# Second attention's preparation moved between the last expert tiles, its bias as one product, and the last layer's norms behind a later split

## What is computed

```
x = x + L0_xattn(layernorm(x), ctx)   # one nearest context row is taken per token
x = x + L0_ffn(layernorm(x))          # 8 experts, top 2 per token, gelu
x = x + L1_xattn(layernorm(x), ctx)   # the "second attention", below
x = x + L1_ffn(layernorm(x))          # the "last layer": experts choose tokens

# L1_xattn, 16 heads of 64
xn = layernorm(x) * gamma + beta
q  = xn @ w_q;  k, v = split(ctx @ w_kv)
o  = softmax(q * 64**-0.5 @ k.T) @ v
return (o @ w_out + b_out) * tanh(gate)
```

## Time and profile before

| | us |
|---|---|
| median of 3 runs (lowest, highest) | 1761.12 (1756.11, 1764.85) |
| profiled execution, its own time | 1759.72 |
| its span in the trace | 1757.8 |
| PE busy (share of the span) | 1659.3 (94%) |
| DVE busy | 1311.6 (75%) |
| ACT busy | 1131.0 (64%) |
| POOL busy | 792.0 (45%) |

### The profile page before, as it was taken

One profiled execution on the slowest core, in us unless ns is written; L12 is line 12 of the kernel. 1 busy time (PEld: TensorE's weight loads), 2 busy tenths in 40 slices (PEclk: granted clock), 3 DMA queues, 4 the chain that ended last, 5 costly groups with the idle time before them and its releaser, 6 DMA issues.

```text
span 1757.8 us, 40697 instructions
## 1 busy us (share of the span) xinstructions
PE 1659.3 (94%) x15617; PEld 1414.3 (80%) x15621; DVE 1311.6 (75%) x2861; ACT 1131.0 (64%) x2880; POOL 792.0 (45%) x1125
## 2 busy tenths in 40 slices
PE   7999999999999999999999879999999999997768
PEld 4677776678788999999999768888888888886656
DVE  5899998461816889888898467878887888767557
ACT  1477776424347778778787467778777877764330
POOL 3245432120012333333331477888788878755300
PEclk9899999899999999999999989999999999999899
DMA  7857565146876677767776722232223222211378
GB/s 207 230 122 152 123 133 147 49 162 231 309 258 223 239 257 247 249 244 246 252 247 236 243 73 64 71 97 71 67 72 95 73 67 68 79 62 49 101 235 291
DMA packets 138770, 283.08 MB, mean 161 GB/s; under 512 B 13808, under 2 KB 89968, under 8 KB 125904
## 3 DMA queue, kind: packets, MB, share of 16 engines
q1 hardware_dynamic: 118176, 168.89, 32.1%
q0 software_dynamic: 20400, 111.59, 18.7%
HBM read 199.03 MB, written 81.13 MB: 159 GB/s over the span
## 4 chain that ended last, share of the span: by engine, by line
PE 70%; DVE 7%; POOL 6%; DMA 5%; issue 5%; ACT 5%; SPq 0%; POOLq 0%; DVEq 0%; ACTq 0%
PE ps L1344 12%; PE ps L1358 11%; PE ps L407 5%; PE ps L2201 5%; PE ps L243 4%; PE ps L2186 3%; PE ps L2224 3%; ACT P L220 3%; PE ps L411 3%; PE ps L500 3%; PE ps L476 3%; POOL P L233 2%; PE ps L488 2%; PE ps L2237 2%; PE ps L576 2%
## 5 line engine op out<-in xcount | busy, mean ns | idle before, releaser
L220 ACT ACTIVATE P<-ps,NM 128x256 f32<-128x256 f32 x512 | 238.0, 495 | 116.4 <-DVE NM L209 116.4
L233 POOL TENSOR_TENSOR P<-P,RS 128x1024 f32<-128x1024 f32 x128 | 244.7, 1918 | 56.4 <-DVE RS L227 55.8
L1344 PE MATMUL ps<-XRP,W1P 128*128 128x256 f32 (+1 forms) x1872 | 226.2, 281 | 3.3 <-DVE W1P L1428 3.3
L1344 PEld LDWEIGHTS ps<-XRP,W1P 128*128 128x128 f32 x1872 | 219.8, 190 | 4.1 <-DVE W1P L1428 3.6
L1358 PE MATMUL ps<-W2P,HP 128*128 128x256 f32 x1704 | 204.2, 278 | 0.0
L1358 PEld LDWEIGHTS ps<-W2P,HP 128*128 128x128 f32 x1704 | 200.3, 188 | 0.0
L642 DVE TENSOR_REDUCE NM<-ps 128x2 f32<-128x512 f32 x256 | 164.4, 684 | 31.0 <-PE ps L476 30.2
L741 ACT ACTIVATE PT<-ps 128x512 f32<-128x512 f32 x256 | 139.2, 597 | 63.8 <-PE ps L488 61.5
L209 DVE TENSOR_REDUCE NM<-ps 128x2 f32<-128x512 f32 x256 | 164.0, 682 | 3.9 <-PE ps L2186 3.1
L1277 POOL DMA_INDIRECT WE<-in_we,WIX x39 | 44.3, 1136 | 265.3 <-DVE W1P L1428 192.2
L243 PE MATMUL ps<-CST,P 128*128 128x128 f32 x1024 | 139.3, 279 | 17.8 <-ACT PT L250 16.7
(11 more groups left out here) (287 smaller groups left out, 3685.6 us busy)
## 6 DMA issues: line engine op xcount, KB each, us to landing
KS<-k_scratch SPq DMA_DIRECT2D x64, 256.0 KB, 3.0
V<-v_scratch SPq DMA_DIRECT2D x16, 1024.0 KB, 6.9
k_scratch<-KVM SPq DMA_DIRECT2D x52, 256.0 KB, 3.2
QS<-q_scratch SPq DMA_DIRECT2D x96, 128.0 KB, 4.5
v_scratch<-KVM SPq DMA_DIRECT2D x40, 256.0 KB, 2.8
ctx_scratch<-CHL SPq DMA_DIRECT2D x32, 256.0 KB, 2.8
CHR<-ctx_scratch SPq DMA_DIRECT2D x16, 512.0 KB, 4.8
ys_scratch<-YS SPq DMA_DIRECT2D x32, 256.0 KB, 7.9
```

Source lines behind the costliest of these rows:

```text
L220: i = e.activation(self.P[u % 4][:, c, :], PS[SB1[n % 4]][:, y * 256:y * 256 + 256], ACT.Exp, bias=self.NM[:, u % 4, c:c + 1], accum_out=s ...
L233: e.tensor_tensor(p, p, self.RS[:, u % 4, :].unsqueeze(2).to_broadcast([128, 4, 256]), ALU.mult).then_inc(self.s_pn, 1)
L1344: m = e.matmul(PS[p][:, hh * 256:hh * 256 + n], W1P[i % 2][wi][:, cc * 1024 + hc * 128:cc * 1024 + hc * 128 + 128], XRP[i % 2][xi][:, cc * ...
```

## The change

- SP issues the loads of gamma and beta (GB), bias (BO), gate (TG) and W1O's source (WT1) in the expert stage, behind the store of expert tile 37 (the next to last), ahead of the last context loads. Before, the first three followed the last ys store and WT1 the last value store. WT1 gets another place in memory.
- ScalarE makes tanh(gate), W1O's high parts and the first two keys' high parts between value tiles 113 to 121. VectorE makes W1O's low parts before the first queries' low part.
- Queries 0 go ahead of tile 127. Queries 1 get a bank of their own and need not wait for the low part of queries 0; their high part is made behind the first slot's exponentials.
- Statistics of batch 1 and two of its adds come earlier. Its norms move from slot 0 to slot 1, its two transposes and scales from slots 0 and 1 to slots 1 and 2; adds and gathers of batches 2 and 3 move accordingly.
- The bias is one product: ROW2 has ones in rows 0 and 32, and the bias's high part lies in row 0 of BOS, the low part in row 32. It is made in slot 1.
- Norm b of the last layer, from b = 5 on, waits for one batch's split more.

```diff
@@ sp_ffn, behind the store of tile NTF - 2
                 w.wait_ge(s_ym, NTF - 1)
+                e.dma_start(GB[:, :, :], A["gb"]).then_inc(d_w0_w1, 16)
+                e.dma_start(BO[:, :], A["bo"].to_broadcast([128, 256])).then_inc(d_w0_w1, 16)
+                e.dma_start(TG[:, 0:1], A["gate"].to_broadcast([128, 1])).then_inc(d_w0_w1, 16)
+                e.dma_start(WT[1][:, :].rearrange("p (a b) -> p a b", a=8), A["w1o"]).then_inc(d_wt_wf2[1], 16)
                 for b in (14, 15):
@@ norm(b), last layer
-            w.wait_ge(s_x3p, 2 * (b - 3))
+            w.wait_ge(s_x3p, 2 * (b - 2 if b > 4 else b - 3))
@@ queries(d), PE
-            w.wait_ge(s_qb, d)
+            w.wait_ge(s_qb, d if d > 2 else d - 1)
             w.wait_ge(s_rb, added)
+            M = queries_bank(d)
@@ result(x), PE
             if half:
-                for j in range(2):
-                    m = e.matmul(M, EYE[:, :], BOS[j][:, :], start=False, stop=(j == 1))
+                m = e.matmul(M, ROW2[:, :], BOS[:, :], start=False, stop=True)
@@ pe_l1
-        for t in range(LATE, 128):
+        for t in range(LATE, 127):
             late_tile(e, w, t)
         w.wait_ge(s_kve, 125)
         queries(0, 0)
-        w.wait_ge(s_kve, 128)
+        late_tile(e, w, 127)
...
+            if i == 2:
+                turn_x(1, 1, split)
+                turned += 1
             for u in turns_in(i)[0:1]:
+                w.wait_ge(s_qb, 2)
                 a1.turn_pe(e, w, u)
...
-            if n < 2 and is_batch(g + 1):
-                turn_x(g + 1, n, split)
+            for b, cc in input_turns(i) if g else ():
+                turn_x(b, cc, split)
                 turned += 1
             for d in queries_in(i)[-1:]:
                 queries(d, results_before(i + 1))
+            if i == 1:
+                turn_x(1, 0, split)
+                turned += 1
@@ bias(), DVE
             w.wait_ge(s_tanh, 1)
-            e.tensor_copy(EYE[:, :], ident).then_inc(s_bo, 1)
+            e.tensor_scalar(ROW2[:, :], ones, ident[:, 0:1], None, ALU.mult).then_inc(s_bo, 1)
             e.tensor_scalar(BO[:, :], BO[:, :], TG[:, 1:2], None, ALU.mult).then_inc(s_bo, 1)
             w.wait_ge(s_bo, 2)
-            e.tensor_copy(BOS[0][:, :], BO[:, :]).then_inc(s_bo, 1)
+            e.tensor_scalar(ROW2[32:64, :], ones[32:64, :], ident[32:64, 32:33], None, ALU.mult)
+            e.tensor_copy(BOS[:, :], BO[:, :]).then_inc(s_bo, 1)
             w.wait_ge(s_bo, 3)
-            e.tensor_tensor(BOS[1][:, :], BO[:, :], BOS[0][:, :].bitcast(fp32), ALU.subtract).then_inc(s_bo, 1)
+            e.tensor_tensor(BOS[32:64, :], BO[32:64, :], BOS[32:64, :].bitcast(fp32), ALU.subtract).then_inc(s_bo, 1)
@@ act_l1
         for t in range(KV_MAIN, LATE):
             late_out(e, w, t)
-        w.wait_ge(d_ys[0], 16 * 20)
...
+            if t == KV_MAIN + 1:
+                w.wait_ge(d_w0_w1, 96)
+                e.activation(TG[:, 1:2], TG[:, 0:1], ACT.Tanh).then_inc(s_tanh, 1)
+            elif t in (KV_MAIN + 4, KV_MAIN + 6):
+                weights_high(1, (t - KV_MAIN - 4) // 2)
+            elif t in (KV_MAIN + 8, KV_MAIN + 9):
+                w.wait_ge(d_ys[0], 16 * 20)
+                w.wait_ge(d_ys[1], 16 * 19)
+                w.wait_ge(s_ye, NTF)
+                keys_high(t - KV_MAIN - 8)
@@ pool_l1
-        newton(e, w, stat1["a", 0], 0, 2, RSTD)
-        for n in range(2):
-            input_low(0, n)
         for j in range(2, 4):
             gather(1, j)
+        newton(e, w, stat1["a", 0], 0, 2, RSTD)
         w.wait_ge(s_w1l, 4 * NTF)
         for n in range(2):
             keys_low(n)
+        for n in range(2):
+            input_low(0, n)
```

More of the change, by code:

```diff
@@ L1522, in build @@
     BO = mem("BO", [128, 256], fp32)
-    BOS = [mem(f"BOS{i}", [128, 256], f32r) for i in range(2)]
-    EYE = mem("EYE", [128, 128], f32r)
+    BOS = mem("BOS", [128, 256], f32r)
+    ROW2 = mem("ROW2", [128, 128], f32r)
     TG = mem("TG", [128, 2], fp32)
@@ L1643, in queries_before, with input_turns, adds_in, gathers_in @@
         return 1 + sum(len(queries_in(x)) for x in range(i))
+    def input_turns(i):
+        g, n = i // 4, i % 4
+        if g == 0:
+            return {1: ((1, 0),), 2: ((1, 1),)}.get(i, ())
+        return ((g + 1, n),) if n < 2 and is_batch(g + 1) else ()
+    def adds_in(i):
+        g, n = i // 4, i % 4
+        n -= g == 0
+        return tuple((g + 2, 2 * n + j) for j in range(2)) if 0 <= n < 2 and is_batch(g + 2) else ()
+    def gathers_in(i):
+        g, n = i // 4, i % 4
+        if g == 0:
+            return {2: ((3, 0), (3, 1)), 3: ((3, 2), (3, 3))}.get(i, ())
+        return tuple((g + 3, 2 * n - 2 + j) for j in range(2)) if n in (1, 2) and is_batch(g + 3) else ()
+    def queries_bank(d):
+        return PS[TB1[0]] if d == 1 else WB
     def result_part(x):
@@ L2378, in dve_l1 @@
             if i == 0:
+                queries_low(1)
+            if i == 1:
                 norms(1, 0)
                 norms(1, 1)
-                queries_low(1)
             for x in results_in(i):
                 result_add(x, results_before(i + 1))
-            if n < 2 and is_batch(g + 1):
-                scale_x(g + 1, n)
-            if n < 2 and is_batch(g + 2):
-                add(g + 2, 2 * n)
-                add(g + 2, 2 * n + 1)
+            for b, cc in input_turns(i) if i != 1 else ():
+                scale_x(b, cc)
+            for b, j in adds_in(i):
+                add(b, j)
             if n == 2 and g < 17:
@@ L2462, in act_l1 @@
                 a1.turn_act(e, w, u, u - 3)
-            for d in queries_in(i)[-1:]:
+            for d in queries_in(i):
                 queries_high(d)
@@ L2510, in pool_l1 @@
             keys_low(n)
+        for n in range(2):
+            input_low(0, n)
         newton(e, w, stat1["a", 1], 2, 2, RSTD)
-        for j in range(4):
+        for j in range(2):
             gather(2, j)
@@ L2519, in pool_l1 @@
                 keys_low(i + 1)
-            if n < 2 and is_batch(g + 1):
-                input_low(g + 1, n)
-            if n in (1, 2) and is_batch(g + 3):
-                gather(g + 3, 2 * n - 2)
-                gather(g + 3, 2 * n - 1)
+            for b, cc in input_turns(i) if i != 1 else ():
+                input_low(b, cc)
+            for b, j in gathers_in(i):
+                gather(b, j)
             if i < SLOTS1:
                 a1.norm_pool(e, w, 2 * i)
+            if i == 0:
+                gather(2, 2)
+                gather(2, 3)
+            if i == 1:
+                input_low(1, 0)
             if n == 2 and g < 17:
```

41 lines of the change are left out of this document (15 added, 26 removed).

## The result

The changed kernel took 1769.65 us (median of 20 runs, 1763.75 to 1774.80), the kernel before 1760.44 us (20 runs beside it, 1751.80 to 1770.09). The ratio of the two is 1.0043, with a 95% interval of 1.0027 to 1.0058: 7.6 us slower (the medians as they stand are 9.2 us apart). The interval lies clear of 1, though the difference is inside the 0.5% that the prediction took as the least that can be told. The time is above the predicted range, and the change went the other way than forecast. The one profiled execution of it has a span of 1769.2 us against 1757.8.

A forecast was written before the change was run, and what follows sets the result against it. The prediction took TensorE's matmul stream as the bound (70% of the chain that ended last). From the profiled 1759.7 us, 1759.7 + 4.9 - 9.6 - 0.3 + 1.1 = 1755.8, so 1756 us, range 1747 to 1764.

The forecast's parts named there:

- Part 1: Start of the second attention: loads ahead of the last ys store delay it 2.3 us; first scores 4.9 us later.
- Part 2: First five slots of the second attention: 42.8 us against 54.1, 11.3 less; 9.6 net of a clock drop.
- S+16.7: S is the start of the second attention's first scores; VectorE was to be free in slot 1 16.7 us later.
- Part 3: Bias as one product in the attention, 32 matmuls fewer: 0.3 us gained, bounds 0 and 1.8.
- Part 4: Norms of the last layer: norm 5 waits for one split more and runs beside another; 1.1 us lost, bounds 0 and 1.9.
- The late store costs nothing: Rival at the attention's start: the last ys store is not delayed, first scores move 0.9 us; 1751.8 us, chance 0.25.
- The third slot eats the gain: Rival in the first slots: bias, norms and input hold exp up, 5 us more; 1761 us, chance 0.14.
- Norm beside split in each batch: Rival in the last layer: each of 11 norms from batch 5 on pays 1.0 us; 1765.7 us, chance 0.07.

The follow-up runs named there:

- e3: The changed kernel with all four loads (GB, BO, TG, W1O) behind the last ys store; ratio 1.0022 to the kernel before.
- h2: The changed kernel with the five bias instructions on VectorE ahead of the first norms; ratio 1.0034 to the kernel before.
- e4: The kernel before with only the four loads moved ahead of the context loads and the last ys store; ratio 1.0053 to the kernel before.
- e6: The changed kernel with only W1O's load behind the last ys store; ratio 1.0021 to the kernel before.
- e5: The changed kernel with only the three small loads (GB, BO, TG) behind the last ys store; ratio 1.0033 to the kernel before.

## Why the prediction was wrong

**The sum.** It had 4.9 - 9.6 - 0.3 + 1.1 = -3.9. By the stretches, with the means of the groups for the last two terms, it was 10.0 - 8.0 + 0 + 3.0 + 3.9 = +8.9, for a measured 7.6 (4.8 to 10.2 by the interval). The gain came nearly as forecast. Of the three losses two were too small in the forecast, and the third, at the end of the program, was not in the list at all.

**Part 1 (4.9, was 10.0).** The mechanism, ring order and no cover at the norm, was right: the loads delay the store, TensorE waits for XN, and the clock falls behind it. The step that failed is "1.05 MB of W1O, 0.13 of the bias and 1.05 of context must pass, 2.23 MB; at 320 GB/s". For W1O the bytes held (1.05 MB at that rate is 3.3 us, and it cost 2.8). The small loads were counted by bytes too, 0.4 us, and cost 4.2; together the store was 6.1 us later, not 2.3. A row of before could have told: the dip to 82 GB/s in 978 to 981, right behind the same three loads, which the prediction did not use. The wait at the norm then was 7.6 us, not 2.8: the gathers, adds and Newton steps lost 1.3 more, and from the norm to the scores passed 11.6 us instead of 9.0, at a granted clock of 0.75. In e3, with the same order of work and a clock of 1.00, it was 9.5, so the new order cost 0.5 and the clock 2.1 (forecast 0.6 and 1.7). The bounds, 0.9 to 8, did not reach 10.0.

**Part 2 (-9.6, was -8.0).** The first two slots came as worked out (6.8 and 6.2 us for 6.7 and 6.1), the fourth and fifth too (8.6 and 8.8 for 9.1 and 8.8), and the clock fell behind the third slot's wait, as said. The third took 15.7 us for 12.1 + 1.7. The step is "VectorE in slot 1 ... is free only at about S+16.7": it was free at S+18.5, since its norms and adds ran beside GpSimd at more than two and a half times their undisturbed lengths, a slowing for which the prediction's sum has no term in this slot. That the bias instructions stand in the wrong place was named, and cost 2.9 us (h2).

**Part 3 (-0.3, was 0 in the steady state and +3.9 at the end).** The seventeen profiles put the steady stretch at 548.8 us on average with either form, so no gain from the loop is shown; the -2.3 of the one profile was chance. What failed is the bound "0 and 1.8": removing an instruction was costed only by its own time. That it moves all code behind it was in no case or rival.

**Part 4 (1.1, was 3.0).** That norm 5 is the one that waits was right, and so was how long: it was done 3.9 us behind the gather instead of 2.0, the forecast 1.9 later. The step "I guess 0.8 of the 1.9 us to be absorbed" asked the wrong question: the wait at TensorE was 0.5 to 1.2 us in seven profiles, as thought, but it came when the clock had just fallen, behind a wait of 2.5 us, and the clock over 12 us was then 0.56 to 0.58 instead of 0.72 to 0.88. Part 1 and part 2 had a term for the clock; part 4 had none.

**The rivals.** "The late store costs nothing" got 0.25 and is refuted by e4. "The third slot eats the gain" was the nearest, for the 2.9 us of the bias instructions, where it had 5. "Norm beside split in each batch" did not occur in the changed kernel but does exist, in six batches (h2). The slower side had 0.07 for one mechanism, where three separate losses each had room to be larger.

## What to carry to other kernels

Cost a transfer on a busy queue by its rows as well as its bytes, and look in the trace for the rate right behind the same load before it is moved. Where TensorE already idles near a clock drop, give one more microsecond of idling a term for the clock beside its own length. When an edit removes instructions far ahead of a stretch of short products, compare that stretch too, and give the same program with the old count as a control before crediting or blaming the edit.

## What the hardware did that I had not expected

- A broadcast of 4 bytes to 128 partitions (TG) took 5.4 us to land beside other work, and with the 128 KB broadcast BO it held the DMA engines to 41 to 49 GB/s for three microseconds with 1 to 2 MB waiting (e6 and the changed kernel); with W1O first in the queue they ran at 338 (e5).
- TensorE's large waits for its own instructions stood at the same matmul counts, multiples of 128 apart, in all variants, up to 4.8 us each, and 81 of 98 ended 1.15 to 1.60 us behind the end of a 16,384-byte instruction packet; 32 matmuls fewer, all of them in the attention before, went with a last part 3.9 us longer on average.
- A TensorE wait of 0.53 to 1.23 us, 4 us behind one of 2.5, went with a granted clock of 0.56 to 0.58 over 12 us in seven profiles, where 0.72 to 0.88 stood in the nine without it; in h2, where the clock had not yet fallen, a wait of 1.61 us left it at 0.86.
- VectorE instructions beside GpSimd's took up to nine times their length (a cast of 0.29 us took 2.58).
